# Softmax sums carried through the transpose banks, GpSimd's long operations placed behind combinations, and other planning numbers, in a transformer layer kernel

## The reference

```python
q = (x @ Wq) ...; k = (x @ Wk) ...; v = (x @ Wv) ...     # 16 query heads, 4 key/value groups
q1, q2, k1, k2 = rope(each half of q and k)
a1 = softmax(q1 @ k1.T * scale + causal mask)
a2 = softmax(q2 @ k2.T * scale + causal mask)
lam = exp(sum(lambda_q1 * lambda_k1)) - exp(sum(lambda_q2 * lambda_k2)) + LAMBDA_INIT
out = (a1 - lam * a2) @ v
out = (out - mean) * rsqrt(var + EPS) * gn_w + gn_b      # mean, var over positions and head columns
x1 = layernorm(x + (out * (1 - LAMBDA_INIT)) @ Wo)
up, gate = x1 @ ternary(W_up).T, x1 @ ternary(W_gate).T
y = layernorm(x1 + (silu(up) * gate) @ ternary(W_down).T)
```

## Time and profile before

| | |
|---|---|
| median of three runs | 2373.8 us |
| the profiled execution itself | 2379.38 us |
| its span, first to last instruction | 2377.6 us |
| mean granted PE clock | 0.987 |
| PE / DVE / ACT / POOL busy | 94% / 75% / 62% / 50% |

### The profile page before, as it was taken

How to read it: one execution, slowest core, us unless ns; L and a number is a source line. 1 busy time by engine, 2 the same in 40 slices (tenths; PEclk the granted TensorE clock), 3 DMA queues, 4 the chain that set the end, 5 groups by cost and what they waited for, 6 DMA issues and landing times.

```text
span 2377.6 us, 41383 instructions
## 1 busy us (share of the span) xinstructions
PE 2234.6 (94%) x13602; PEld 1396.8 (59%) x13602; DVE 1776.1 (75%) x3829; ACT 1478.3 (62%) x3554; POOL 1199.2 (50%) x1883
## 2 busy tenths in 40 slices
PE   8798988988999999999999999999999999999998
PEld 4565656565666666666666665566656666644444
DVE  3687888889787878877878878888867878842343
ACT  1476757575666767767667767677757767731232
POOL 0465655657644646645545645564544545621232
PEclk9899999999999999999999999999999999999999
DMA  6767645485733222412432312232242211112000
GB/s 208 238 197 215 190 152 184 163 241 178 214 101 85 72 75 64 131 43 73 150 98 81 94 53 86 87 119 67 82 128 73 61 45 59 54 32 84 1 18 18
DMA packets 257604, 256.53 MB, mean 108 GB/s; under 512 B 31344, under 2 KB 199408, under 8 KB 255216
## 3 DMA queue, kind: packets, MB, share of 16 engines
q1 hardware_dynamic: 246016, 220.26, 30.5%
q10 hardware_dynamic: 11376, 33.63, 4.5%
HBM read 182.53 MB, written 71.30 MB: 107 GB/s over the span
## 4 chain that ended last, share of the span: by engine, by line
PE 69%; DVE 13%; issue 7%; DMA 4%; POOL 3%; ACT 3%; SPq 1%; ACTq 0%; DVEq 0%; POOLq 0%
PE F L1018 15%; PE PV L957 10%; PE F L1005 9%; PE S L940 8%; PE F L1027 8%; PE F L985 8%; PE F L925 7%; DVE e_long L1268 4%; PE PV L960 2%; DVE e_long L1346 2%; DMA wt<-in_w_gate 1%; PE F L993 1%; DVE e_short L1346 1%; ACT e_long L1078 1%; POOL linv L1207 1%
## 5 line engine op out<-in xcount | busy, mean ns | idle before, releaser
L1207 POOL TENSOR_TENSOR linv<-lsum,powers 128x2 f32<-128x2 f32 x512 | 414.3, 809 | 707.3 <-ACT e_long L1078 567.2
L1078 ACT ACTIVATE e_long<-e_long,nmax 128x768 f32<-128x768 f32 (+3 forms) x512 | 505.4, 989 | 159.0 <-DVE nmax L1268 157.7
L1268 DVE CUSTOM_DVE_ANT_0 e_long<-S,mask_b 128x768 f32<-128x768 f32 (+3 forms) x512 | 512.1, 1019 | 100.1 <-PE S L940 97.5
L940 PE MATMUL S<-kstk,qstk 128*128 128x384 f32 (+5 forms) x1536 | 508.3, 424 | 55.5 <-DVE nmax L1268 46.2
L940 PEld LDWEIGHTS S<-kstk,qstk 128*128 128x128 f32 x1536 | 278.5, 195 | 190.5 <-DVE nmax L1268 80.9
L1071 ACT ACTIVATE dt_long<-F 128x512 f32<-128x512 f32 (+3 forms) x512 | 239.9, 511 | 173.1 <-PE F L925 168.6
L1346 DVE SCALAR_TENSOR_TENSOR e_long<-e_long,coef 128x1024 f32<-128x1024 f32 (+3 forms) x256 | 309.7, 1210 | 46.9 <-POOL coef L1208 46.0
L985 PE MATMUL F<-xT,wr 128*128 128x512 f32 x640 | 304.1, 607 | 2.9 <-DVE t L1303 0.8
L1078 ACT ACTIVATE e_short<-e_short,nmax 128x384 f32<-128x384 f32 (+3 forms) x512 | 284.3, 559 | 29.5 <-DVE nmax L1268 28.7
L1268 DVE CUSTOM_DVE_ANT_0 e_short<-S,mask_b 128x384 f32<-128x384 f32 (+3 forms) x512 | 237.8, 486 | 64.7 <-PE S L940 62.1
L925 PE MATMUL F<-ident,e_long 128*128 128x128 f32 x1664 | 237.8, 276 | 16.3 <-DVE e_long L1346 12.5
(11 more groups left out here) (108 smaller groups left out, 3357.2 us busy)
## 6 DMA issues: line engine op xcount, KB each, us to landing
qstk<-dq SPq DMA_DIRECT2D x512, 128.0 KB, 2.8
dq<-hl SPq DMA_DIRECT2D x32, 1024.0 KB, 5.5
wr<-in_w_proj ACTq DMA_DIRECT2D x48, 512.0 KB, 4.5
kstk<-dk SPq DMA_DIRECT2D x64, 256.0 KB, 5.0
da<-ra SPq DMA_DIRECT2D x32, 512.0 KB, 3.1
at_sb<-da SPq DMA_DIRECT2D x32, 512.0 KB, 4.0
dk<-hl SPq DMA_DIRECT2D x8, 1024.0 KB, 5.5
wt<-in_w_up SPq DMA_DIRECT2D x16, 512.0 KB, 4.9
```

The costliest lines, as they stand in the source:

```text
L940: last = nc.tensor.matmul(slot[:, h, :], qstk[:, duo % 4, 2 * r + m, :].bitcast(F32R), kstk[:, g % 2, m, h * w:(h + 1) * w].bitcast(F32R), ...
L1078: nc.scalar.activation(e, e, ACT.Exp, bias=nmax[:, u % 8:u % 8 + 1], scale=-1.0, accum_out=lsum[:, n % 4, m:m + 1]).then_inc(s_exp, 1)
L1207: link(nc.gpsimd.tensor_tensor(linv[:, a % 8, :], lsum[:, a % 4, :], mone, ALU.pow))
L1268: nc.vector.tensor_tensor_reduce(out, slot, mask, -1.0, -NEG, ALU.add, ALU.min, nmax[:, u % 8:u % 8 + 1]).then_inc(s_negmax, 1)
```

## The change

Six things are changed together.

1. The inverse sums no longer pass through PV. They are one more 128x128 block of the `turn` of the duo's second head (r = 1), behind that head's last key blocks, in the same F bank. For an even duo the block lands in `dt_long[1]` behind the key blocks with the same copy; for an odd duo a second ACT copy brings it to `r_short`. Where the key blocks fill their banks (t = 7 and t = 3) the block is a `turn` of its own: 64 more of them. `inverses`, `r_sb` and the third buffer of `wide` are gone; DVE's `product` waits for `values` alone. An `evict` of a second head waits also for the product of two duos before.
2. Each long POOL operation (`rotate` and `low`, now two instructions each that may stand apart, the group norm's last scaling, now an item `settle` of its own, and `hidden low`) waits until DVE has done the combination of the last head whose `factor` stands ahead of it on POOL (`combined`).
3. Margins: `HAND_OVER` falls from 0.3, 0.5, 0.4 to 0.2, 0.3, 0.2 for PE, ACT and POOL; costs of `values`, `rotate`, `low` and others are set anew.
4. The first four rotated pairs: the sums and the high and low part on DVE are an item of their own (`early`).
5. The rotary table is loaded in two halves with a semaphore each, both ahead of the second weight load; the second load of keys waits until head 8's scores are done.
6. `store rotated` gets a weight of 3.0 on SP.

```diff
 def turns(n):
 
-    return STEPS[n].t // 4 + 1
+    return (STEPS[n].t + STEPS[n].r) // 4 + 1
...
+KEYS_AT = 8
...
-HAND_OVER = {"pe": 0.3, "act": 0.5, "dve": 0.2, "pool": 0.4}
+HAND_OVER = {"pe": .2, "act": .3, "dve": .2, "pool": .2}
 LANDS = {"load q": 3.1, "load k": 5.5, "load v": 4.5, "store v": 3.9, "store rotated": 5.2, "store a": 3.5, "load a": 4.4,
-         "store out": 2.5, "load wo": 4.0, "load x1": 6.0, "load weight": 4.5, "load x": 3.7, "load w": 4.2, "load rope": 6.0, "load lambda": 5.0, "load first": 2.5}
+         "store out": 2.5, "load wo": 4.0, "load x1": 6.0, "load weight": 4.5, "load x": 3.7, "load w": 4.2, "load rope": 5.0, "load lambda": 5.0, "load first": 2.5}
 
 
...
 def blocks_of(n, half):
-    return min(4, STEPS[n].t + 1 - 4 * half)
+
+    t, r = STEPS[n].t, STEPS[n].r
...
+        out = [stored(a // KV, 1, 0)]
+        if a:
+            out.append(ITEM("scores", 32 * (a - 1) - 1 if a >= 2 else KEYS_AT, 1))
     elif what == "load v":
```

```diff
+LONG = ("rotate", "low", "settle", "hidden low")
...
                 r = max([r] + [end[other] for other in others])
                 if item.what == "scores" and item.a and item.b == 0:
                     r = max(r, end[ITEM("scores")] + PACE * item.a)
+                if item.what in LONG and factors:
+                    other = ITEM("combine", factors - 1)
+                    if other not in end:
+                        continue
+                    r = max(r, end[other])
...
+        if what in LONG:
+            held[item] = factors
+        if what == "factor":
+            factors = a + 1
...
             def evict(n, half):
-                blocks = min(4, STEPS[n].t + 1 - 4 * half)
+                blocks, keys = blocks_of(n, half)
+                duo = STEPS[n].duo
                 bank, _ = BANK_OF[ITEM("turn", n, half)]
                 act.wait_ge(s_tb, TURN[n, half] + 1)
                 back = n - (6 if n % 2 else 4)
                 if half == 0 and back >= 0:
                     act.wait_ge(s_pv, STEPS[back].duo + 1)
-                nc.scalar.activation(dt_of(n)[:, 4 * half:4 * half + blocks, :].rearrange("p k q -> p (k q)"),
-                                     F[bank][:, 0:blocks * P], ACT.Copy).then_inc(s_ffree[bank], 1)
+                if half == 0 and STEPS[n].r and duo >= 2:
+                    act.wait_ge(s_pvfree, duo - 1)
+                here = blocks if n % 2 == 0 else keys
+                if here > 0:
+                    copied = nc.scalar.activation(
+                        dt_of(n)[:, 4 * half:4 * half + here, :].rearrange("p k q -> p (k q)"), F[bank][:, 0:here * P], ACT.Copy)
+                if here < blocks:
+                    copied = nc.scalar.activation(r_short[:, :], F[bank][:, here * P:blocks * P], ACT.Copy)
+                copied.then_inc(s_ffree[bank], 1)
 
             def exponent(n, m):
                 e = e_of(n, m)[:, 0:(STEPS[n].t + 1) * P]
@@ -1125,11 +1160,6 @@
                     exponent(a, b)
                 elif what == "evict":
```

```diff
-                for k in range(min(4, STEPS[n].t + 1 - 4 * half)):
+                blocks, keys = blocks_of(n, half)
+                for k in range(keys):
                     col = (4 * half + k) * P
                     last = nc.tensor.transpose(F[bank][:, k * P:(k + 1) * P], e1_of(n)[:, col:col + P], ident[:, :])
+                if blocks > keys:
+                    duo = STEPS[n].duo
+                    pe.wait_ge(s_wide, duo + 1)
+                    last = nc.tensor.transpose(F[bank][:, keys * P:blocks * P],
+                                               wide[:, duo % 2, :, :].rearrange("p r d -> p (r d)"), ident[:, :])
                 last.then_inc(s_tb, 1)
 
             def scores(n, m):
@@ -954,11 +983,9 @@
                     pe.wait_ge(s_pvfree, duo)
                 for kb in range(t + 1):
                     for r, n in enumerate((first, second)):
-                        nc.tensor.matmul(PV[64 * r:64 * r + 64, 0:P], vkv[:, g % 2, kb, :], dt_of(n)[:, kb, :],
-                                         start=kb == 0, stop=kb == t)
-                pe.wait_ge(s_wide, duo + 1)
-                nc.tensor.transpose(PV[:, P:2 * P], wide[:, duo % 3, :, :].rearrange("p r d -> p (r d)"), ident[:, :])\
-                    .then_inc(s_pv, 1)
+                        last = nc.tensor.matmul(PV[64 * r:64 * r + 64, 0:P], vkv[:, g % 2, kb, :], dt_of(n)[:, kb, :],
+                                                start=kb == 0, stop=kb == t)
+                last.then_inc(s_pv, 1)
 
             def fill(job, piece):
                 which, use = BANK_OF[job]
...
                     if STEPS[a].r:
-                        if duo >= 3:
-                            pool.wait_ge(s_pv, duo - 2)
-                        nc.gpsimd.tensor_copy(wide[:, duo % 3, :, :], linv[:, (a - 2) % 8:a % 8 + 1:2, 0:1]
+                        if duo >= 2:
+                            second = heads_of(duo - 2)[1]
+                            pool.wait_ge(s_tb, TURN[second, turns(second) - 1] + 1)
+                        nc.gpsimd.tensor_copy(wide[:, duo % 2, :, :], linv[:, (a - 2) % 8:a % 8 + 1:2, 0:1]
                                               .broadcast_to((P, 2, 64))).then_inc(s_wide, 1)
                 elif what == "hidden low":
                     f, eb = HID[a], a.i % 8
+                    combined(ITEM("hidden low", a))
                     pool.wait_ge(s_hhi, f + 1)
                     nc.gpsimd.tensor_tensor(hid[:, 1, eb, :], th[:, f % NTH, :], hid[:, 0, eb, :], ALU.subtract)\
...
-                    nc.gpsimd.tensor_tensor(t4[:, 1, :], t4[:, 1, :], t4[:, 3, :], ALU.add).then_inc(s_rot, 1)
+                    combined(ITEM("rotate", a, b))
+                    if b == 0:
+                        freed(pool, a)
+                        nc.gpsimd.tensor_tensor(t4[:, 0, :], t4[:, 0, :], t4[:, 2, :], ALU.subtract)
+                    else:
+                        nc.gpsimd.tensor_tensor(t4[:, 1, :], t4[:, 1, :], t4[:, 3, :], ALU.add).then_inc(s_rot, 1)
                 elif what == "low":
-                    pool.wait_ge(s_hi, ROT[a] + 1)
-                    nc.gpsimd.tensor_tensor(hl[:, 2:4, :], t4[:, 0:2, :], hl[:, 0:2, :], ALU.subtract).then_inc(s_lo, 1)
+                    combined(ITEM("low", a, b))
+                    if b == 0:
+                        pool.wait_ge(s_hi, ROT[a] + 1)
+                        nc.gpsimd.tensor_tensor(hl[:, 2, :], t4[:, 0, :], hl[:, 0, :], ALU.subtract)
+                    else:
+                        nc.gpsimd.tensor_tensor(hl[:, 3, :], t4[:, 1, :], hl[:, 1, :], ALU.subtract).then_inc(s_lo, 1)
                 elif what == "group":
                     c = a % 8
                     pool.wait_ge(s_gve, a + 1)
@@ -1239,6 +1284,8 @@
                     link(nc.gpsimd.tensor_tensor(gsm[:, 5:6], gsm[:, 4:5], gn_sb[:, 0, c:c + 1], ALU.mult))
                     link(nc.gpsimd.tensor_tensor(gsm[:, 6:7], gsm[:, 0:1], gsm[:, 5:6], ALU.mult))
                     link(nc.gpsimd.tensor_tensor(gsm[:, 7:8], gn_sb[:, 1, c:c + 1], gsm[:, 6:7], ALU.subtract))
+                elif what == "settle":
+                    combined(ITEM("settle", a))
...
                 elif what == "high":
                     high_part(ROT[a])
                 elif what == "product":
                     t, chunk = STEPS[heads_of(a)[0]].t, a // 8
-                    dve.wait_ge(s_rcopy, a + 1)
+                    rows = r_short[:, :] if a % 2 else dt_long[1][:, t + 1, :]
+                    dve.wait_ge(s_pv, a + 1)
                     if a % 8 == 0 and chunk >= 2:
                         dve.wait_ge(s_rast[chunk % 2], 16 * (chunk // 2))
-                    nc.vector.tensor_tensor(ra[:, chunk % 2, t * P:(t + 1) * P], PV[:, 0:P], r_sb[:, :], ALU.mult)\
+                    nc.vector.tensor_tensor(ra[:, chunk % 2, t * P:(t + 1) * P], PV[:, 0:P], rows, ALU.mult)\
```

124 lines of the change are left out of this document (63 added, 61 removed).

## The result

| | before | changed |
|---|---|---|
| median | 2374.16 us (2371.05 to 2379.49, 9 runs) | 2379.48 us (2373.91 to 2382.04, 9 runs) |
| profiled execution, its span | 2379.38, 2377.6 us | 2373.91, 2372.1 us |
| TensorE's mean granted clock | 0.987 | 0.989 |

The ratio is 1.0022, with a 95% interval of 1.0012 to 1.0031. The forecast was 2338 us, 41 us less, and the time lies outside the range of 2314 to 2374. The change made the kernel a little slower. The profiled execution of the changed kernel is the fastest of its nine runs and that of the kernel before the slowest of its nine, so the spans of the two traces stand in the other order (5.5 us shorter). Traces are used here for where time goes, and the medians for how much.

A forecast was written before the change was run, and what follows sets the result against it. PE was taken as the bound, its idle time and clock as winnable. Opening 7.5, collisions 12, clock 9, inverse sums 4, margins 8, holds -5 sum to 35.5 us: median 2338 from 2373.8, range 2314 to 2374.

The forecast's parts named there:

- What the holds cost: POOL's long operations wait, delaying next factors, and late low parts keep DVE from E products: -5 us, ends 0 and -40.
- R3: Rival: holds put 115 us onto POOL's path to rotated operands, a third reaching PE; slower, 2394 us; chance 0.12.
- more than 55 us of idle time before 660: Sign of a wrong forecast: PE's idle time before 660 us, 68.3 us in the profile, stays above 55.
- The opening: First query load: earlier store removes most of PE's 6.5 us wait and the low clock around it: 7.5 us, ends 0 and 8.6.
- Collisions: DVE combinations held by long POOL operations: eight PE waits, 14.4 us, go; gain 12 us, ends 6 and 20.
- the reservation made in the prediction: POOL's factors read SBUF too and can still hold a DVE combination; the change leaves that, and no price was put on it.
- The clock: PE's granted clock up to 660 us: with fewer bunched waits, 9 us of lost work return, ends 0 and 18.
- Inverse sums: ACT's 256 copies from PV go and DVE's product needs PE alone: 4 us reach PE, ends 0 and 12.
- hardly waiting before the product: Expected in the later profile: DVE, which stood 53.3 us before the product for ACT's copy, would hardly wait there.
- PE's waits on ACT's copies come to the head of the list: Sign of a wrong forecast: waits on ACT's copies lead the list of PE's waits; no size given.
- Margins: Smaller planning margins move consumers closer to producers in all lists: 8 us of second-stage idle time, ends -15 and 20.
- The sum: All terms added, 7.5 + 12 + 9 + 4 + 8 - 5 = 35.5 us gained: median 2338 us; forecast's chance 0.50.

The follow-up runs named there:

- e1: The changed kernel with the old HAND_OVER margins (0.3, 0.5, 0.2, 0.4) and all else as changed: 2392.7 us, 1.0089 to the kernel before.
- e3: The changed kernel without the rearranged first loads and the weight on stores of rotated tiles; rotary table still in halves: 2397.3 us, 1.01 to before.
- e7: The changed kernel with the planning constant PACE at 3.98 instead of 4.0, another order of the same work: 2384.9 us, 1.0048 to before.
- e15: The changed kernel with the planning constant PACE at 4.02 instead of 4.0, another order of the same work: 2377.6 us, 1.0023 to before.
- e5: The changed kernel with every list as it is, only POOL's waits for combinations on the chip taken out: 2398.7 us, 1.0109 to before.
- e2: The changed kernel without the holds, in the plan and on the chip; long POOL operations stay split: 2363.4 us, 0.9959 to before.
- e10: The changed kernel without holds (e2), with the planning constant PACE at 3.98 instead of 4.0: 2379.4 us, 1.003 to before.
- e4: The changed kernel with inverse sums again through PV and an ACT copy; margins, holds and opening as changed: 2378.9 us, 1.003 to before.
- e17: The changed kernel without holds and with inverse sums again through PV, PACE 4.0; new margins and opening stay: 2354.6 us, 0.992 to before.
- e18: The same kernel as e17 with the planning constant PACE at 3.98 instead of 4.0: 2361.1 us, 0.9949 to before.

## Why the prediction was wrong

**The step that failed** is "What the holds cost": -5, ends 0 and -40. It was priced as waiting on the chip (POOL late, hence late low parts and DVE standing at the next E product). POOL does wait, 141 us ahead of the rotated pieces (R3 had put 115 there), but that does not reach the engine it was priced for: DVE's wait for the low part went from 5.1 to 1.7 us, far from the 40 at which rival R3 was to decide.

```profile
L1349 DVE SCALAR_TENSOR_TENSOR t<-F,cs 128x512 f32<-128x512 f32 x80 | 54.9, 687 | 42.2 <-PE F L1012 37.6 <-issue 2.3 <-POOL hl L1279 1.7
```

What the step left out is the planner. The hold is there too: it lets `rotate` and `low` start only after a combination, which puts low parts later, and with them the E and O jobs. In all eight kernels with held rotated pieces (the changed one, e1, e3 to e7 and e15) 408 to 480 E and O matmuls had begun by 660 us; in the twelve others 512 to 552. A sum over PE's timeline says what that means. Each instruction begun by then is counted at what it takes when it follows its like without a gap: 0.11 us for a transpose (eight in 1.04 us above, less 0.27 for the first, by seven), 0.43 for an E or O matmul, 0.22 for one of a V job, 0.11 for a pair of `values`, and for scores their columns by 2.4 GHz. This estimate gives some 502 us of work by 660 us in the kernel before. It is 11 us less in the changed kernel and 7 to 29 us less in the seven others that hold rotated pieces, and 3 to 20 us more in each of the eleven others that don't. Thus were read too simply. A shorter list of waits isn't more work done: "busy" counts each transpose at 0.27 us though it needs 0.11 when others follow, so the lists' thin stretches show up as busy. The whole of PE's work is some 2030 us by this count, of 2235 us busy. The first sign that the prediction named for being wrong, more than 55 us of idle time before 660, came: 74.2 us.

Net, the holds cost 12 us over three orders. In the order where both sides were measured their lists cost 35.3 us (e5 less e2, neither of which waits on the chip) and their waits give 19.2 of it back (e5 less the changed kernel). That the deficit by 660 us is how the lists cost is inferred from the counts; no run changed that alone, and e10 shows that more work by then doesn't settle the end (some 15 us ahead, 2379.4 us).

**The opening** (7.5): right in mechanism. The store went out at 47.78 (49.3 expected), scores at 60.61 (60.8 to 63), the clock between 70 and 80 us is 1.00 instead of 0.79. Undoing it cost 18 us, with a median clock of 0.980 instead of 0.985, in one order. So the size is known no better than between a few us and 18.

**Collisions** (12): the combinations came out as worked out (0.81 us, none above 2), PE's waits behind them fell further than the 50 us expected, and in the fixed lists of the changed kernel their absence gives 19 us (e5), inside the ends. As the change buys it, it costs more than that. The rule of the Trainium skill (SBUF — State Buffer, "Who interferes with whom"), that the second of the two is blocked entirely, agrees with the trace for the long operations: the combination at 310.06 ended 0.4 us after POOL's. For the factors the trace does not bear it out, against the reservation made in the prediction. 40 combinations of the changed kernel begin while a factor's first operation (0.80 us on average) is running by the trace; they take what undisturbed ones take, none over 0.01 us more.

**The clock** (9): the wrong sign. The profiled execution has 0.97 instead of 0.96 up to 660 us, where 0.98 or more was expected, but it had the highest mean clock of its nine runs, 0.989. Their median is 0.985, and that of the 85 runs of the kernel before in the experiments is 0.988: some 7 us of PE's work lost (estimate, as above). The dip at the earlier trace rows's second stretch stayed (0.66 for 0.57).

**Inverse sums** (4): the ACT copy went, but the waits did not. DVE "hardly waiting before the product" was expected, and it waits 52.2 us instead of 53.3: by the trace it is mostly PE's values that hold the product, and not the copy. The sign was wrong too: 0 with the holds in, a loss of 9 to 18 us without. Only what disappears was priced; the block's longer way through the three shared banks was not. "PE's waits on ACT's copies come to the head of the list" was named as a sign of failure, and it came, but with the held lists rather than with this part: 44.8 us in all, 38.6 with the inverse sums back in PV (e4), 22.1 without holds (e2); 31.6 to 47.6 in the eight kernels that hold rotated pieces, 6.8 to 25.2 in the twelve others.

**Margins** (8, ends -15 and 20): 13 us in one order (e1), inside the ends. Margins and opening together, with the other two parts undone (and with the split POOL operations and the `early` item, which no run took back), give 2354.6 and 2361.1 at 4.0 and 3.98 (e17, e18) against 2374.2 and 2365.3 before: 12 us, about what was asked of them (15.5), and much less than the 31 us that e1 and e3 make when added.

**The sum.** Its terms were added as if each wait removed shortened the end. The measured account over the two paces run for all stages is 12 us gained (margins and opening), 14 lost to the inverse sums, 11 lost to the holds: about -12, where +35.5 stood. How the last two share their loss depends on which is added first: at 4.0 the holds alone cost 24.3 us (e4 less e17), after which the inverse sums add 0.6. R3 had the right sign and the right part, and its waits of POOL, but they did not reach PE by the way it gave.

Still open: what inside the inverse sums' new way costs, why its loss vanishes under the holds, and how much of the holds' loss comes by the later E and O jobs. Holds on the chip under lists planned without them were not tried.

## What to carry to other kernels

A change to a planned order is two changes: the wait on the chip and all lists that the planner draws anew. Compare how much work each list has done by some fixed time, not only the waits that a profile names, and compare the granted clock of all runs, not of the one that was profiled. Before a difference under about 15 us is given a cause here, draw the order a few times with a constant moved by half a per cent. Where an operation that is removed had a wait ahead of it, ask where that wait will stand next. Where a reader of a DMA shares its engine with the copies that free PE's banks, a later planned landing is worth a try: it went with a gain in three pairs of three.

## What the runs showed of the hardware

A combination of 1024 columns takes 1.28 us and one of 128 takes 0.35 when no long GpSimd operation meets it, and 71 us of 488 went on such meetings. In fixed lists taking them away gave 19 us (e5 against the changed kernel). Short GpSimd operations, the factors of 128x2, lengthened no combination that began beside them. A weight piece of the feed-forward part landed at medians of 4.5 to 6.2 us in the changed kernel, for 4.5 in its table: ACT stood up to 7.5 us for one of them, and such waits came to 38.7 us there.
